# Self and causal attention of a fused decoder on Trainium2: the value projection as one plain fp32 product instead of three rounded ones

## The reference

```
x = x + self_attention(layernorm(x))        # 16 heads of 8, rotary positions by position
x = x + cross_attention(layernorm(x), ctx)  # keys and values from ctx
x = x + experts(layernorm(x))               # top 2 of 8 and 2 shared
x = x + causal_attention(layernorm(x))      # rotary by position, causal mask
x = x + latent_attention(ctx, layernorm(x))
x = x + experts(layernorm(x))               # top 2 of 8
# in an attention:
q = h @ Wq + bq;  k = h @ Wk + bk;  v = h @ Wv + bv      # h = layernorm(x)
out = softmax(q k^T / sqrt(8)) v;  out @ Wo + bo
```

## Time and profile before

| what | value |
|---|---|
| median of 3 runs | 1343.76 us (1337.65 to 1350.34) |
| the profiled execution's own time | 1335.86 us |
| its span, first to last instruction | 1333.8 us |
| PE, PEld busy | 1108.2 us (83%), 825.9 us (62%) |
| DVE, POOL, ACT busy | 887.8 (67%), 792.0 (59%), 675.6 us (51%) |

### The profile page before, as it was taken

The page is one execution under the profiler, slowest core; times in us unless marked ns, Lnnn a source line. Parts: engine busy times, 40 slices in busy tenths (PEclk is TensorE's granted clock), DMA queues, the critical chain, the costliest instruction groups (busy, mean ns, idle before and its releaser), DMA issues. The chain is left out here.

```text
span 1333.8 us, 30226 instructions
## 1 busy us (share of the span) xinstructions
PE 1108.2 (83%) x10619; PEld 825.9 (62%) x10619; DVE 887.8 (67%) x2152; ACT 675.6 (51%) x1304; POOL 792.0 (59%) x895
## 2 busy tenths in 40 slices
PE   1799997788888886899969999993799886599992
PEld 0566665555555556566636766662788885488881
DVE  3588887579999994766536777764799886322223
ACT  1355554435545442455425565645888653255551
POOL 4788875546555552444446766743888676754542
PEclk9999998679999997799979999995999887699996
DMA  9930000000000000000000000000000002376665
GB/s 345 381 112 2 2 2 7 9 15 16 16 22 15 10 10 1 0 1 1 1 0 2 2 2 2 2 2 19 13 13 8 13 26 78 114 216 199 195 188 192
DMA packets 51556, 75.20 MB, mean 56 GB/s; under 512 B 13118, under 2 KB 31683, under 8 KB 51152
## 3 DMA queue, kind: packets, MB, share of 16 engines
q1 hardware_dynamic: 43344, 60.57, 14.4%
q0 software_dynamic: 4544, 8.47, 1.9%
q10 hardware_dynamic: 3520, 4.23, 0.9%
HBM read 40.37 MB, written 31.70 MB: 54 GB/s over the span
## 5 line engine op out<-in xcount | busy, mean ns | idle before, releaser
L626 DVE TENSOR_REDUCE maxes<-bank 128x8 f32<-128x1024 f32 x192 | 233.6, 1217 | 52.1 <-PE bank L418 51.2
L553 ACT ACTIVATE self_probs<-bank 128x1024 f32<-128x1024 f32 x128 | 129.0, 1022 | 45.2 <-PE bank L450 44.7
L1521 POOL DMA_INDIRECT returned<-relu_y,relu_slots x78 | 76.3, 979 | 68.4 <-DVE relu_y L1497 55.0
L1458 ACT ACTIVATE relu_hidden<-bank,cols 128x256 f32<-128x256 f32 x156 | 73.8, 473 | 77.1 <-PE bank L1417 77.1
L784 POOL TENSOR_TENSOR self_k_hi_m<-self_kq_hi,const 128x512 fp32r<-128x512 f32 x64 | 66.5, 1039 | 74.8 <-ACT self_kq_hi L581 74.8
L560 ACT ACTIVATE self_neg_max<-bank 128x512 fp32r<-128x512 f32 x64 | 38.2, 596 | 133.2 <-PE bank L463 133.2
L1417 PE MATMUL bank<-latent_kq,relu_w_tile 128*128 128x256 f32 x312 | 94.8, 387 | 0.5 <-DVE latent_kq L1491 0.5
L1425 PE MATMUL bank<-relu_hidden,relu_w_tile 128*128 128x256 f32 x312 | 93.1, 381 | 0.0
L1491 DVE COPY latent_kq<-bank 128x256 f32<-128x256 f32 x39 | 16.6, 425 | 100.2 <-PE bank L1407 100.2
L632 DVE TENSOR_SCALAR bank<-bank 128x1024 f32<-128x1024 f32 x64 | 78.2, 1224 | 3.3 <-PE bank L438 3.3
L2402 POOL DMA_INDIRECT routed<-latent_rows,latent_place_i x64 | 62.6, 979 | 24.4 <-issue 22.2
(11 more groups left out here) (402 smaller groups left out, 3432.8 us busy)
## 6 DMA issues: line engine op xcount, KB each, us to landing
relu_w_tile<-in_w_ffn SPq DMA_DIRECT2D x39, 512.0 KB, 3.7
routed<-blank SPq DMA_DIRECT2D x1, 19760.0 KB, 61.2
relu_slots<-routed SPq DMA_DIRECT2D x39, 130.0 KB, 3.1
x_all<-in_x SPq DMA_DIRECT2D x8, 256.0 KB, 8.3
x_before<-x_all SPq DMA_DIRECT2D x8, 256.0 KB, 2.3
relu_back<-returned SPq DMA_DIRECT2D x4, 512.0 KB, 8.0
latent_mask_rows<-returned ACTq DMA_DIRECT2D x4, 512.0 KB, 8.5
self_ctx_in<-in_ctx SPq DMA_DIRECT2D x8, 192.0 KB, 2.4
```

Of the source, the lines that this page charges most:

```text
L553: act.activation(probs[n % 2][:, 2 * pair:2 * pair + 2, :, :].rearrange("p u j q -> p (u j q)"), T[:, 2 * pair * GT:(2 * pair + 2) * GT], ...
L626: dve.tensor_reduce(out.rearrange("p j u -> p u j"), S.rearrange("p (u j k) -> p u j k", u=2, j=U), AX.X, ALU.max, negate=True).then_inc(m ...
L1458: act.activation(hidden[i % C1][:, :], HT[i % 2][:, 0:TT], ACT.Relu, bias=sb["cols"][:, bass.ds(r + (COL_RELU + c), 1)]).then_inc(hidden_d ...
L1521: pool.indirect_dma_start(returned[:, :], bass.IndirectOffsetOnAxis(ap=slots[t % NX][:, b, P:P + 1].bitcast(I32), axis=0), y[t % NY][:, b, ...
```

## The change

The values of self and causal attention are made by one plain fp32 product per block from `x_whole`, an unrounded copy of PB that ACT makes just before `x_hi`, and from `w_value`, an unsplit copy of the value weights. A plain fp32 product stands in the trace as two loads and two products. `x_whole` is made in every group, the cross attention's too; its values are still made from the split context. `w_value` is a fifth load of ACT's queue in the setup, and DVE waits for it as well.

```diff
@@ load_setup
             act.dma_start(sb["w_out"][:, :].rearrange("p (a c) -> p a c", c=P), w_out).then_inc(rows_in, 16)
+            w_value = weights.rearrange("p (a n c) -> p a n c", n=len(AW), c=P)[:, :, AW.index("v"), :]
+            act.dma_start(sb["w_value"][:, :].rearrange("p (a c) -> p a c", c=P), w_value).then_inc(rows_in, 16)
...
-            dve.wait_ge(rows_in, 64)
+            dve.wait_ge(rows_in, 80)
@@ attention
+    def value_weight(G):
+        c = ATT[of_group(G)] * P
+        return sb["w_value"][:, c:c + P]
...
+        x_whole = buf("x_whole", [P, GT])
@@ project
-                if name == "v":
+                if name == "v" and not from_context:
+                    for b in range(GB):
+                        cols = slice(b * P, (b + 1) * P)
+                        mm = pe.matmul(PB[:, cols], x_whole[:, cols], value_weight(G), start=True, stop=True)
+                elif name == "v":
                     for b in range(GB):
@@ round_inputs
                 act.wait_ge(x_transposed, G + 1)
+                act.activation(x_whole[:, :], PB, ACT.Copy)
                 act.activation(x_hi[:, :], PB, ACT.Copy).then_inc(x_hi_done, 1)
@@ decoder
+                "w_value": buf("w_value", [P, 3 * P]),
```

## The result

The changed kernel takes 1352.6 us (median of 13 runs, 1337.93 to 1360.33) beside 1341.77 us for the kernel before (13 runs on the same chip, 1332.64 to 1350.34). The ratio is 1.0089 [1.0058, 1.0119]: slower by 0.9%. I had forecast 1344.2 us, in practice no change, with a range of 1336 to 1352. The profiled execution is the slowest of the thirteen, 1360.33 us with a span of 1358.5, 0.6% above the median, and that of the kernel before was 0.4% under its median, so the two traces lie 24.7 us apart where the medians differ by 10.8.

The account below looks back on a forecast made before the run. PE was taken to bound causal, PE or DVE self, DVE cross. Setup +1.3, self -0.35 + 0 + 2.0, way into cross +0.5, cross 0, causal -0.35 + 0 - 2.7 sum to +0.4 us: 1344.2, range 1336 to 1352.

Parts of the forecast that it names:

- The setup: Fifth load, `w_value`, lands behind `w_out` and delays DVE's first instruction and everything after: +1.3 us.
- the price of a record: PE value projection: a record costs the same in both forms, 0.112 us; four fewer save 0.45 us per group.
- cross groups: Six steady cross groups: the first exponential ends 0.50 us later but is covered by ACT's idle time; cost 0.
- the way in: First cross group: the negative maximum's copy stands behind the rounding on ACT and PE waits for it; +0.5 us.
- the wait of `T` in self: Self groups: `T` on PE waits for the exponentials about 1.2 us instead of 0.85.
- the covers of the copy in causal: Causal: the copy's 0.50 us delay of `x_lo` and the exponential is covered by 0.37 and 1.08 us; cost 0 to 0.13.
- The steady causal groups: Six steady causal groups: PE's saving shows in full, 0.45 us each, 2.7 us in all.
- The saving that reaches a self group: Self: PE's next scores wait for DVE, so of 0.45 us only 0.17 can be had, ACT reaching the rounding earlier.
- steady self groups: Six steady self groups: copy's 0.50 us delays `T` without cover, less 0.17 saved: 0.33 us each, +2.0 in all.
- The first group: First causal and first self group, lower clock: 0.85 us saved against 0.50 for the copy, -0.35 each.
- each second group: Second group of self and of causal attention: saving and copy cost taken as even, 0.
- rival C: PE's clock stays low a few us more or less; forty records are 4 us, so 1340 to 1348; 12%.

Follow-up runs that it names:

- the kernel that takes the collision away: Kernel before plus fp32 values in the last six causal and self groups, copy behind the exponential, load awaited by PE, POOL's self low parts in four pieces: 1341.55 us, 1.0011.
- the repeat: The whole change, unaltered, timed and traced a second time against the kernel before: 1350.15 us, ratio 1.0054.
- causal without its first groups: Kernel before plus fp32 values in the last six causal groups only, copy there behind the exponential, load awaited by PE alone: 1336.88 us, ratio 0.9977.
- first causal groups only: Kernel before with the fp32 value product, low parts left out, in the first two causal groups alone: 1348.41 us, ratio 1.0072.
- twice: Kernel before with the fp32 value product in the first two causal groups alone, low parts left out, each product made twice: 1343.85 us, ratio 1.0036.
- held: Kernel before with fp32 values in the first two causal groups alone, low parts left out, first causal scores waiting for an unused ACT copy: 1339.74 us, 0.9997.
- copy-only: Kernel before with the unused copy `x_whole` ahead of `x_hi` in all 24 groups, no load, values as before: 1352.47 us, ratio 1.0075.
- copy-behind: Kernel before with the unused copy in self and causal, behind the exponential (first two groups of each: ahead of `x_hi`): 1340.79 us, ratio 1.0018.

## Why the prediction was wrong

**Right.** The setup (+1.27, I had 1.3), the price of a record (eight in 0.88 us from first to last start, I had 0.85), cross groups at 0, the way in at +0.49 (0.5), the wait of `T` in self (1.17, I had 1.2), the covers of the copy in causal. The steady causal groups give 0.37 to 0.40 us, where I had 0.45. The saving that reaches a self group is 0.15 to 0.17 us and not 0.45, as argued: the kernel that takes the collision away shows it. (That 0.17 came out exactly is partly luck: the rows beside it give 134.76 - 134.55 = 0.21.) The eight records take 0.03 us more than forecast because the first distance is 0.21 and not 0.17.

The section "TensorE Precision Notes" of the Trainium skill's page "FP8 and Floating Point Precision" has true FP32 take four passes and says nothing of fp32r, so it doesn't price the exchange: the eight records of four blocks took less than the twelve that they replace, 0.88 us against 1.28.

**A term mis-sized: steady self groups.** I wrote "DVE waits at the same place and can't catch up" and so +0.33 a group. Measured: +0.55. DVE doesn't only wait at the same place; moved by the 0.5 us, its `shares` meets POOL's low-part instruction and is held until that ends. That DVE then sets the time is shown by its reduction, which waits no more for PE. The size fits, as an estimate: the 0.49 that the delay of `T` cost, less the 0.15 that reached the group without collision, is the forecast +0.33, and `shares` is the other 0.2. I had looked at what each engine waits for by semaphores, and at no instruction whose duration could change. The trace of before held the case itself, inside the chain of DVE that I read as unbroken; its timeline there:

```profile
129.96 1.05 POOL L784 TENSOR_TENSOR self_q_hi_m<-self_kq_hi,const 128x512 fp32r<-128x512 f32 x1
...
130.30 0.86 DVE L645 TENSOR_TENSOR self_shares<-self_by_query,self_per_query 128x128 f32<-128x128 f32 x1
```

POOL's instruction ends at 131.01 and `shares` at 131.16, after 0.86 us, where it takes 0.29 with POOL idle (125.39). The rule was to be had: the Trainium skill, page "SBUF — State Buffer", section "SBUF: two separate sides", says that VectorE with two inputs in SBUF and GpSimd take the shared ports as "an exclusive lock, not a bandwidth split". By that rule the trace agrees, with ends 0.15 us behind POOL's.

**The step that failed: the first groups and the clock.** "The first group runs at the lower level: 0.85 saved", less 0.50 for the copy, so -0.35, and "In each second group I take the two as even". The first of these holds: from the first rounding to the second it is 16.10 us in self and 14.17 in causal, 16.36 and 14.42 before, -0.25 each. The second fails, because the sum left the clock's rise where it was. From the second causal rounding to the third it is 30.75 us, and 27.40 in the repeat's trace, where before had 23.37. The two first causal groups together cost 7.1 us in the one trace, 3.8 in the other. With the fp32 form in them the rise came 31.8 to 43.9 us after the first rounding, in four traces of four; with the three products 19.4 to 20.0 us after it, in eight of eight. I had the clock as rival C, with 12% and 4 us to either side, sized by "Forty records more or fewer" at 0.10 us. Measured, the rise is put off by 12 to 24 us in causal, and in the trace after it also came late in two other places.

**The sum anew.** Without the clock: 1.3, two first groups at -0.25 (-0.5), six self groups at 0.55 (3.3), way in 0.5, six causal at -0.4 (-2.4): +2.2 us, by 1.8 more than my +0.4. For the clock, the median over all executions is 0.910 against 0.918 to 0.920: 2 x 0.009 x 1350 = 24 us more at the lower level. Where the traces show the price of such time, it is 8.3 us for 24 (first causal groups), about 0.35 us for one, so 8.4. Together some +11, an estimate, and the two sets of runs gave +12 (1.0089) and +7 (1.0054).

**What stays open.** The late rises in self and on the way into cross. In self the rise came at 81.1 and 65.7 us in the two profiled executions of the changed kernel (in the second it fell again from 72.5 to 79.3), but at 74.0 with only the load, and at 72.6 in the kernel whose self code is that of before; in the ten other traces between 52.5 and 60.4. Between groups 7 and 12 it spent 64.9 and 58.0 us at the lower level in those two executions, and 47.8 in before. But of the kernels whose self and cross attention is that of before, one had 47.8 as well (causal without its first groups), and the three others 58.0, 64.9 and 58.0 (first causal groups only, twice, held). So a late rise comes by chance too, and one or two traces a kernel can't tell what the load's shift and the copy add to it. The copy probably has a share, since by the median the copy-only kernel has the clock 0.007 lower and costs 10 us, of which its self groups explain 6; the copy-behind kernel has neither loss. That is argued, not shown. Nor do the runs show why a place 0.75 us earlier goes with a late rise in causal, or how much of the whole change's loss the first causal groups make: without the fp32 form there and in self's first groups it is still at 1.0043.

## What to carry to other kernels

Moving a step on one engine by half a microsecond also moves what the next engine's two-input instructions meet on GpSimd: before costing a delay, look at which of them run close to a GpSimd instruction, and place new work behind the step that others wait for instead of ahead of it. Leave the groups that run while TensorE is at its lower clock alone, or measure them by themselves: here 0.75 us saved there cost over 8. And where a clock can rise early or late, compare the granted clock over all executions: the traces of the twice kernel and of before end 20.2 us apart, their medians differ by 3.1.

## What the runs showed of the hardware

- A VectorE multiplication with two inputs in SBUF, started while a GpSimd instruction of two inputs ran, ended 0.15 us after it in all four kernels shown (0.86 us in before, 1.14 with the copy, 1.40 with the product, 0.90 with both), and took 0.29 us with GpSimd idle. With the GpSimd instruction cut into four it ended 0.15 us after the first piece and took 0.31, though the four take 1.77 us instead of 1.29.
- TensorE's clock stayed at the lower level (0.50) through a stretch with 12.00 of 12.00 us busy in the changed kernel, and in the held kernel it rose after 19.8 us, with 14.63 of the first 20 busy.
- Records of plain fp32 products of 128 columns stood 0.11 us apart (changed kernel, from 816.78), and so did those of fp32r (before, from 814.90); only the first distance differed, 0.21 and 0.17.
